# ScalarE's search rounds with absolute values and signs, and the last rounds of one VectorE tile moved to ScalarE

## The reference

```python
logits = Q @ W2 @ K.T / TAU
idx = jnp.argsort(-logits, axis=1)
vals = jnp.take_along_axis(logits, idx, axis=1)
csum = jnp.cumsum(jax.nn.softmax(vals, axis=1), axis=1)
k_i = jnp.sum(csum < P_NUC, axis=1) + 1
...
masked = jnp.where(keep, logits, -jnp.inf)
return jax.nn.softmax(masked, axis=1)
...
for s in range(STEPS):
    A = _adj_from_feats(Xa, W1, W2, W3)
    Xf = Rf @ Xf
    Xb = Rb @ Xb
    Xa = A @ Xa
    Z = Z + (Xf @ U1[s] + Xb @ U2[s] + Xa @ U3[s])
```

## Time and profile before

| what | value |
|---|---|
| median of 3 runs | 3786.09 us (3783.11 to 3787.79) |
| span of the profiled execution | 3781.4 us |
| step 0, from ScalarE's first round to `take_over` | 73.8 to 1531.6 us |
| step 1, the same | 1625.5 to 3074.3 us |
| VectorE busy | 94% of the span |
| ScalarE busy | 83% of the span |
| TensorE matmul busy | 78% of the span |

### The profile page before, as it was taken

One profiled execution on the slowest core, in us unless ns is written; L12 is line 12 of the kernel. 1 busy time (PEld: TensorE's weight loads), 2 busy tenths in 40 slices (PEclk: granted clock), 3 DMA queues, 4 the chain that ended last, 5 costly groups with the idle time before them and its releaser, 6 DMA issues. The chain is left out here.

```text
span 3781.4 us, 42418 instructions
## 1 busy us (share of the span) xinstructions
PE 2942.2 (78%) x14004; PEld 2083.2 (55%) x14004; DVE 3553.9 (94%) x4740; ACT 3150.2 (83%) x4561; POOL 360.3 (10%) x417
## 2 busy tenths in 40 slices
PE   6568787786878787648879797888979734799998
PEld 4456666575756666413535354453535424567787
DVE  7999999999999999699999999999999996777887
ACT  6999999999999999389999999999999952345443
POOL 3000000000000000000000000000000005434444
PEclk9689888898989888869989898998989867899999
DMA  2112122212222220032111111111111005355553
GB/s 92 64 55 87 61 93 65 94 54 85 71 78 81 67 87 17 29 133 63 35 41 49 37 46 35 54 37 51 37 41 49 21 5 193 111 176 187 195 205 108
DMA packets 157483, 292.05 MB, mean 77 GB/s; under 512 B 14480, under 2 KB 87248, under 8 KB 153936
## 3 DMA queue, kind: packets, MB, share of 16 engines
q1 hardware_dynamic: 128032, 216.33, 18.2%
q10 hardware_dynamic: 29232, 73.02, 5.5%
HBM read 236.34 MB, written 52.95 MB: 77 GB/s over the span
## 5 line engine op out<-in xcount | busy, mean ns | idle before, releaser
L693 DVE SCALAR_TENSOR_TENSOR s_dump<-s_rows,s_mid 128x3327 bf16<-128x3327 f32 x608 | 2238.8, 3682 | 2.3 <-issue 0.7
L642 ACT ACTIVATE s_adump<-s_rows,s_mid 128x3327 int8<-128x3327 f32 x324 | 995.6, 3073 | 10.6
L648 ACT ACTIVATE s_adump<-s_rows,s_mid 128x3327 int8<-128x3327 f32 x324 | 992.0, 3062 | 0.0
L905 PE MATMUL bank<-x,s_slab 128*128 128x512 f32 x1352 | 633.6, 612 | 0.0
L882 PE MATMUL bank<-kh,qs 128*128 128x512 f16 (+1 forms) x364 | 146.9, 404 | 361.6 <-DVE s_rows L672 351.1
L905 PEld LDWEIGHTS bank<-x,s_slab 128*128 128x128 f32 x1352 | 266.4, 198 | 280.8 <-issue 268.9
L949 PE MATMUL bank<-hb,s_wT 128*128 128x256 f32 x1352 | 356.9, 409 | 69.8 <-ACT s_wT L520 69.7
L949 PE MATMUL bank<-xab,s_wT 128*128 128x256 f32 x1352 | 348.6, 402 | 70.5 <-ACT s_wT L520 70.4
L938 PE MATMUL bank<-ident,s_rows 128*128 128x128 f32 x1352 | 230.5, 298 | 187.3 <-DVE s_rows L747 186.5
L905 PE MATMUL bank<-hb,s_slab 128*128 128x257 f32 x1352 | 353.3, 402 | 0.0
L949 PEld LDWEIGHTS bank<-hb,s_wT 128*128 128x128 f32 x1352 | 261.6, 204 | 119.9 <-ACT s_wT L520 54.2
(11 more groups left out here) (180 smaller groups left out, 4713.8 us busy)
## 6 DMA issues: line engine op xcount, KB each, us to landing
s_slab<-adjT_dram SPq DMA_DIRECT2D x104, 448.0 KB, 4.0
s_slab<-adjT_dram SPq DMA_DIRECT2D x104, 384.0 KB, 3.7
e_adj<-adjR_dram ACTq DMA_DIRECT2D x23, 1664.0 KB, 7.3
strip<-adjR_dram SPq DMA_DIRECT2D x52, 448.0 KB, 3.5
strip<-adjR_dram SPq DMA_DIRECT2D x52, 384.0 KB, 3.3
e_ring<-sc_d SPq DMA_DIRECT2D x72, 256.0 KB, 5.9
sc_d<-e_stage SPq DMA_DIRECT2D x60, 256.0 KB, 2.4
su_d<-s_su_out ACTq DMA_DIRECT2D x26, 256.0 KB, 2.0
```

Of the source, the lines that this page charges most:

```text
L642: nc.scalar.activation(adump[:], row(g, r), ACT.Sign, bias=st(mid, g, 2), accum_out=cnt[:]).then_inc(S["a_eval"], 1)
L648: nc.scalar.activation(adump[:], row(g, r), ACT.Relu, bias=st(mid, g, 2), accum_out=gap[:]).then_inc(S["a_eval"], 1)
L693: nc.vector.scalar_tensor_tensor(out=dump[:], in0=row(g, r), scalar=st(mid, g, r), in1=row(g, r), op0=ALU.is_gt, op1=ALU.mult, accum_out=s ...
L905: ins = nc.tensor.matmul(acc, slab[:, i % NSLAB, j - PIECES[p], :], s_op[:, j, 0:SN], start=False, stop=(j == NT - 1))
```

## The change

ScalarE's second pass sums abs(x - mid) in place of relu(x - mid), so that `base` is no longer needed: its part is now in `rest` = 0.8 Z, which is written once per tile. `fac` moves behind the second pass, `mean` behind `sgn`, and the second fill moves from before `sgn` to after the new `mid`. ScalarE's own tile is now tile 1 and VectorE's are 0 and 2. Of tile 2 VectorE does the first HAND = 19 - TAIL rounds; ScalarE does the last TAIL rounds (1 in step 0, 2 in step 1) at the start of the next group, ahead of its own tile. A group of ScalarE so has BOTH = 19 + TAIL rounds, and its 38 beats are spread over 2 x BOTH half rounds. The third `exponent` of a group stands after these rounds. VectorE's last TAIL rounds of tile 0 run without a partner. The load order is 0, 2, 1 and the buffers of the tiles (`home`) follow it.

```diff
+TAIL = (1, 2)
...
-    return [r for r in ((1, 0) if g == LAST else (2, 0, 1)) if r in roles(g)]
+    return [r for r in (0, 2, 1) if r in roles(g)]
...
+    HAND = BISECT - TAIL[s]
+    BOTH = BISECT + TAIL[s]
+    LAST_TAKE = 2 * BISECT - 1
...
+    def first_take(g):
+        return LAST_TAKE - 9 * len(roles(g + 1))
...
+            def begin(g):
+                act.wait_ge(S["exp_done"], LOADS.index((g, 1)) + 1)
+                if g >= 1:
+                    act.wait_ge(S["a_mid"], BOTH * g)
+                nc.scalar.activation(rest[:, 0:1], st(Z, g, 1), ACT.Copy, scale=2.0 * P_NUC - 1.0).then_inc(S["a_begun"], 1)
+                nc.scalar.activation(less[:, 0:1], st(Z, g, 1), ACT.Copy, scale=-LEAST * 2.0 ** LOG_STEP).then_inc(S["a_begun"], 1)
+                act.wait_ge(S["a_begun"], 4 * g + 2)
+
+            def take_on(g):
+                act.wait_ge(mid_ready[1], HAND * (g + 1))
+                nc.scalar.activation(rest[:, 1:2], st(Z, g, 2), ACT.Copy, scale=2.0 * P_NUC - 1.0).then_inc(S["a_begun"], 1)
+                nc.scalar.activation(less[:, 1:2], st(mid, g, 2), ACT.Copy, scale=-1.0).then_inc(S["a_begun"], 1)
+                act.wait_ge(S["a_begun"], 4 * g + 4)
+
+            def side(it, low, scale, out):
+                last = -1.0 if it + 1 == BISECT else 1.0
+                nc.scalar.activation(out[:], low, ACT.Copy, scale=last * scale).then_inc(S["a_fac"], 1)
+
+            def search(g, r, it, n, first, second):
+                k = r - 1
                 up, down = rate(it)
-                last = -1.0 if it + 1 == BISECT else 1.0
-                nc.scalar.activation(base[:], st(mid, g, 2), ACT.Identity, scale=float(N), bias=st(target, g, 2)).then_inc(S["a_base"], 1)
-                nc.scalar.activation(fac[:], st(mid, g, 2), ACT.Copy, scale=last * (down - up) / 2).then_inc(S["a_fac"], 1)
-                nc.scalar.activation(mean[:], st(mid, g, 2), ACT.Copy, scale=last * (down + up) / 2).then_inc(S["a_fac"], 1)
...
+                low = less[:, k:k + 1]
+                nc.scalar.activation(adump[:], row(g, r), ACT.Sign, bias=low, accum_out=cnt[:]).then_inc(S["a_eval"], 1)
+                first()
                 act.wait_ge(S["a_eval"], 2 * n + 1)
+                nc.scalar.activation(over[:], cnt[:], ACT.Identity, scale=low, bias=rest[:, k:k + 1]).then_inc(S["a_over"], 1)
+                nc.scalar.activation(adump[:], row(g, r), ACT.Abs, bias=low, accum_out=gap[:]).then_inc(S["a_eval"], 1)
+                side(it, low, (down - up) / 2, fac)
                 act.wait_ge(S["a_over"], n + 1)
                 act.wait_ge(S["a_eval"], 2 * n + 2)
-                nc.scalar.activation(sgn[:], gap[:], ACT.Sign, scale=-2.0, bias=over[:]).then_inc(S["a_sgn"], 1)
+                nc.scalar.activation(sgn[:], gap[:], ACT.Sign, scale=-1.0, bias=over[:]).then_inc(S["a_sgn"], 1)
+                side(it, low, (down + up) / 2, mean)
                 act.wait_ge(S["a_sgn"], n + 1)
                 act.wait_ge(S["a_fac"], 2 * n + 2)
-                nc.scalar.activation(st(mid, g, 2), sgn[:], ACT.Identity, scale=fac[:], bias=mean[:]).then_inc(S["a_mid"], 1)
+                nc.scalar.activation(st(mid, g, r) if it + 1 == BISECT else low, sgn[:], ACT.Identity,
+                                     scale=fac[:], bias=mean[:]).then_inc(S["a_mid"], 1)
+                second()
                 act.wait_ge(S["a_mid"], n + 1)
...
+                    lead = 2 * TAIL[s]
+                    twice = 3 * NGRP + 1 - lead
...
+                return due(h, 0, 2 * (BOTH if g else BISECT), 2 * BISECT)
...
-                    when = (20, 29, 37)[-len(roles(g + 1)):]
-                    if b in when:
-                        exponent(3 * (g + 1) + when.index(b))
+                    for p in range(len(roles(g + 1)) - 1):
+                        if b == first_take(g) + 12 + 9 * p:
+                            exponent(3 * (g + 1) + p)
...
+                if g >= 1:
+                    take_on(g - 1)
+                    for it in range(HAND, BISECT):
+                        search(g - 1, 2, it, BOTH * (g - 1) + TAIL[s] + it, next_fill, next_fill)
+                    exponent(3 * g + len(roles(g)) - 1)
+                begin(g)
+                for it in range(FIRST_PART if g == LAST else BISECT):
+                    search(g, 1, it, BOTH * g + it, next_fill, next_fill)
...
             def take_over():
-                dve.wait_ge(S["a_mid"], BISECT * LAST + FIRST_PART)
+                dve.wait_ge(S["a_mid"], BOTH * LAST + FIRST_PART)
...
+                    dve.wait_ge(S["a_mid"], BOTH * g + (BOTH if r == 2 else BISECT))
...
             def between(g, b):
                 if g >= 1 and b == 2:
+                    cut(g - 1, 1)
+                if g >= 1 and b == 3:
+                    scale(3 * (g - 1))
+                    scale(3 * (g - 1) + 1)
+                if g >= 1 and b == 2 * TAIL[s] + 3:
                     cut(g - 1, 2)
...
+            begin(0, 0)
             for g in range(LAST):
-                begin(g, 0)
                 for it in range(BISECT):
...
+                    evaluate(g, it, 0)
+                    if it == 0:
+                        begin(g, 2)
+                    if 1 <= it <= HAND:
+                        move(g, it - 1, 2)
+                    if it >= HAND:
+                        between(g, 2 * it)
+                        judge(g, it, 0)
+                        between(g, 2 * it + 1)
+                        move(g, it, 0)
+                        continue
+                    judge(g, it, 0)
+                    between(g, 2 * it)
+                    evaluate(g, it, 2)
+                    move(g, it, 0)
+                    judge(g, it, 2)
+                    between(g, 2 * it + 1)
+                begin(g + 1, 0)
                 cut(g, 0)
-                move(g, BISECT - 1, 1)
-                cut(g, 1)
...
                 if e == 2:
+                    cut(LAST - 1, 1)
...
+                if e == 2 * TAIL[s] + 3:
                     cut(LAST - 1, 2)
```

More of the change, by code:

```diff
@@ L389, in layer_step @@
             sb(tag + n, [P, 6], F32) for n in ("nb", "Z", "target", "mid", "hit", "mass", "kept", "rk"))
-        cnt, gap, base, over, sgn, fac, mean = (sb(tag + n, [P, 1], F32) for n in ("cnt", "gap", "base", "over", "sgn", "fac", "mean"))
+        cnt, gap, over, sgn, fac, mean = (sb(tag + n, [P, 1], F32) for n in ("cnt", "gap", "over", "sgn", "fac", "mean"))
+        rest, less = (sb(tag + n, [P, 2], F32) for n in ("rest", "less"))
         u12 = sb(tag + "u12", [P, KC, 2 * D], F32)
@@ L486, in exponent @@
                                      accum_out=st(Z, g, r)).then_inc(S["exp_done"], 1)
[L488 to L492, removed]
@@ L637, in _, with next_fill @@
             for g in range(TRIPLES):
[L638 to L644, removed]
-                        fill(g, b)
[L646 to L652, removed]
+                half = 0
+                def next_fill():
+                    nonlocal half
+                    for b in beats(g, half):
+                        fill(g, b)
+                    half += 1
+                if g >= 1:
[6 more added lines that the diff above has]
+                    search(g, 1, it, BOTH * g + it, next_fill, next_fill)
+            for b in range(beats(LAST, half - 1)[-1] + 1, 2 * BISECT):
                 fill(LAST, b)
@@ L685, in evaluate, with so_far @@
+            def so_far(g, it, r):
+                return HAND * g + it if r else BISECT * g + it
             def evaluate(g, it, r):
-                n = BISECT * g + it
+                n = so_far(g, it, r)
                 if it == 0:
-                    dve.wait_ge(begun[r], 2 * (g + 1))
+                    dve.wait_ge(begun[r // 2], 2 * (g + 1))
                 else:
-                    dve.wait_ge(mid_ready[r], n)
-                if n + r >= 1:
-                    dve.wait_ge(mass_done[1 - r], n + r)
+                    dve.wait_ge(mid_ready[r // 2], n)
+                if r == 2:
+                    dve.wait_ge(mass_done[0], so_far(g, it, 0) + 1)
+                elif it == 0 and g >= 1:
+                    dve.wait_ge(mass_done[0], n)
+                elif 1 <= it <= HAND:
+                    dve.wait_ge(mass_done[1], so_far(g, it, 2))
@@ L707, in alone @@
+                nc.vector.tensor_scalar(st(mid, g, r), st(hit, g, r), rate(it)[1], st(mid, g, r), ALU.add, ALU.mult).then_inc(mid_ready[r // 2], 1)
             def alone(it):
@@ L800, in between @@
                 if g >= 1 and b == 2:
+                    cut(g - 1, 1)
[3 more added lines that the diff above has]
+                if g >= 1 and b == 2 * TAIL[s] + 3:
                     cut(g - 1, 2)
-                if g >= 1 and b == 3:
-                    for q in roles(g - 1):
-                        scale(3 * (g - 1) + q)
+                if g >= 1 and b == 2 * TAIL[s] + 4:
+                    scale(3 * (g - 1) + 2)
                 if s == 0 and g >= 1:
@@ L818, in between @@
```

(22 more changed lines are left out.)

52 lines of the change are left out of this document (24 added, 28 removed).

## The result

The changed kernel takes 3914.35 us (median of 4 runs, 3910.2 to 3915.67), before it is 3785.62 us in the same measurement. The ratio is 1.0338, with a 95% interval from 1.0324 to 1.0353: slower by 3.4%. Its profiled span is 3908.1 us, 126.7 us above the span of before. The forecast was 3895 us, and 109 us more span.

The account below looks back on a forecast made before the run. VectorE set the pace before, ScalarE almost full; after, ScalarE's chain ends last: (31 - 12) + (100 - 8 - 2.3) = 109 us more span, 3890, and with the median 4.7 us above the span 3895 us; range 3855 to 3922.

Parts of the forecast that it names:

- The bound: At every `take_over`: ScalarE's chain, 31 us longer in step 0 and 100 in step 1, ends last, VectorE's gets shorter.
- the signs I had named: ScalarE over 97% busy per group, groups about 175 and 181 us, VectorE idle 4 to 18, `take_over` wait 10 to 20.
- VectorE's side: Rounds of tile 0 without a partner: 8 in step 0, 16 in step 1, 83 us less on VectorE, perhaps 92.
- ScalarE's round: Empty round from 7.71 to 7.62 us, with both fills from 7.52 to about 7.28; rounds add 27 and 96 us.
- The waits taken back: ScalarE's waits for TensorE, half taken back: 12 of 23.4 us in step 0, 8 of 16.9 in step 1.
- Where VectorE waits: VectorE idle 4 to 18 us per group, nearly all at `cut` of tile 1, waiting for ScalarE's `mid`.
- the rival in which ScalarE and TensorE hold each other: Logits, transposes and `item` reach ScalarE's fills late: 2 us in each of 16 groups, 32 us more, 3927; chance 0.10.
- The absolute pass: ScalarE's second pass: 3.06 us, as for L648 and the exponential, with one table load; table-load rival 4677 us, chance 0.01.
- The rule on which engine: Skill's rule, add and max to VectorE: a moved round costs 7.71 us on ScalarE, 3.85 on VectorE, twice what it frees.

## Why the prediction was right

**The bound.** Right. ScalarE's chain ends last: VectorE waits for it, or for TensorE's logits, in every group of both steps but the first, and 9.9 and 26.0 us at the two ends. One more pass on VectorE in each group cost nothing, and eight rounds less on ScalarE gave back their full length. Of the signs I had named, ScalarE's share of a group is 97.8% in step 0 but 96.3% in step 1 (over 97), the groups take 177.1 and 183.7 us (175 and 181), and VectorE is idle for 8.7 and 23.2 us of them (4 to 18). They miss to the same side as the time: the chain is longer than I had worked out, by 18 us of span, and the rest of the 19 us up to 3914 is that the median of the runs stands 6.3 us above the span here and 4.7 before.

**VectorE's side.** I expected 83 to 92 us less and the page has 92 (3553.9 to 3461.9). As worked out, none of it shows.

**ScalarE's round.** The empty round was put at 7.62 us and has 7.62, but by two errors that cancel. The first: `over` starts 0.22 us behind the read, not 0.29. The second: `sgn` to the new threshold is 0.48 us, not 0.40. `mean` starts 0.20 behind `sgn`, and the threshold follows it by 0.28 us; I had taken 0.22 from a copy followed by a pass. That the empty round is right is therefore luck. In a round with fills only the second counts, for there the read's wait is hidden. So the filled round came out too cheap (7.28 where the timeline has 7.35 without the fills themselves), and this is the term that was mis-sized: step 0, where 270 of 324 halves held a fill before, has 41.8 us more in its rounds where I had 31; step 1 has 105.7 where I had 100.

**The waits taken back.** I took half. Step 0 gave back 16.7 of 23.4 us, more than my 12; the waits for the first transposes went almost wholly (13.4 to 2.1 us). Step 1 gave back 3.2, and 2.6 behind its DMA issues, less than my 8. Together 22.5 against 20: the size was right and the place wrong, which is luck as well, for the half was a guess. The terms, with 1.1 us more of exponentials in each step, make 26 for step 0 where I had 19, and 99 for step 1 where I had 90; 2 us lie outside the steps.

**Where VectorE waits.** Wrong. I expected it at `cut` of tile 1, for ScalarE's threshold. It waits elsewhere: in step 0 as long at `kl`, for ScalarE's `s_q` (24.8 us), as at `take` for logits (24.1), and in step 1 only at `take`, up to 20.2 us at a time. TensorE's program has transposes, their products and logits in one order of beats, and in step 1 it waits 199.2 us for ScalarE to evacuate, where it waited 70.4 before; so ScalarE's lateness reaches VectorE through TensorE. The rows fit this reading, but no run changed TensorE's order to show it. It is near the rival in which ScalarE and TensorE hold each other, but not that rival: ScalarE's own waits for TensorE fell, to 6.1 us in step 0 and 15.2 in step 1. Nor did VectorE's waits cost anything, as the run with more work on VectorE shows: VectorE has the time.

**The absolute pass.** 3.06 us, as taken, and one table load in the whole trace. The Trainium skill (ScalarE: Activation LUTs, Table sets) has abs in every set, and the trace agrees: no load stands between the signs and absolute values of 348 rounds and the exponentials.

**The rule on which engine.** That a moved round costs twice what it frees held: 7.6 us of ScalarE (the run with TAIL = (1, 1)) for 3.5 to 3.85 of VectorE. It is the second pass that makes it so: for a single pass over 128 x 3327 f32 with a sum, ScalarE is the faster one here, 3.06 us against VectorE's 3.68. That the trace agrees, as the prediction says, holds for a round and not for a pass. Nor is twice the price the whole answer. With four moved rounds of eight in step 0 the same trade was a gain, because ScalarE's time was idle and VectorE's was not; in step 1 it gained nothing, and there VectorE waits 14.1 us for logits, as much as the four rounds were to bring.

## What to carry to other kernels

Before work is moved to an engine with a lower busy share, count how much of its idle time is waiting for others, and compare that with one whole unit of the moved work: here 5 us per group against 7.6. If the unit is larger than the slack of one period, try it in every second period: two groups can share the slack, as in step 0 here, but three, four and five of eight differ by 4 to 9 us a step, and in step 1 none of them gained. A busy share over the whole span doesn't name the engine that sets the pace; work added to a suspect engine does, in one run. And measure a control that has every change but the one in question, since here a new order of work alone made some 9 of the 24 us. In a chain of small dependent operations, removing one is worth only what it did not cover, and the independent ones belong where a result is being waited for: moving one of them was worth 47 us, and the whole new round, with one operation less but that one in the wrong place, 27.

## What of the hardware was not expected

On ScalarE an operation that depends on the one before starts after a time that depends on the pair: 0.22 us behind the read of the sign pass for `over`, 0.28 behind a copy for the new threshold, 0.33 behind `sgn` for the same, 0.42 behind the threshold for the next pass. One number for all of them was wrong by up to 0.07 us, which 348 rounds made visible.

A DMA issue of ScalarE's queue directly behind a short operation can hold up the next one. In the changed kernel the fill that takes the `zu` product starts 0.45 us behind the new threshold, where fills without a DMA in front of them start at 0.29:

```profile
570.19 0.39 ACT L533 ACTIVATE s_less<-s_sgn,s_mean,s_fac 128x1 f32<-128x1 f32 x1
570.22 0.33 ACTq L591 DMA_DIRECT2D su_d<-s_su_out  x1
570.64 0.60 ACT L597 ACTIVATE s_zu_out<-bank 128x512 f32<-128x512 f32 x1
```

There are some 20 of these in step 0, 13 at 0.45 us and 8 at 0.40, 3 us in sum; in all of them the issue starts 0.02 to 0.03 us behind the threshold. Where it starts 0.08 us or more behind, the next fill still starts at 0.29, and a pass starts at 0.42 with an issue in front of it or without. That the queue's issue is the cause is read from the timeline; no run took it away.
